# Second layer's depthwise convolution: 52 of 196 taps on GpSimd, VectorE's partial sums in PSUM, three query groups between the chunks

## The reference

```python
x_ln = layernorm(x, ln_g, ln_b)
q = x_ln @ wq + bq                                  # query image, one per channel
o = conv_general_dilated(q_img, dw_w, (2, 2), [(3, 3)] * 2, feature_group_count=c)   # 7x7, depthwise, stride 2
o = gelu(o + dw_b)                                  # 16x16 points
offsets = 1x1 conv of o with pw_w                   # 2 numbers a point
grid = tanh(offsets) and the reference points
interp = bilinear samples of x at grid              # 256 points
k, v from interp; q again through mq_w; attention; mo_w; residual; layernorm; mlp_w; gelu; residual
```

## Time and profile before

| | |
|---|---|
| time, median of 3 runs | 4248.88 us (4244.26 to 4249.75) |
| the profiled execution | 4248.9 us, span 4247.2 us |
| mean granted clock of TensorE | 0.984 of full |
| busy: TensorE, VectorE, ScalarE, GpSimd | 4062.9, 2985.9, 2580.8, 1303.4 us |
| VectorE's taps (L1537), 880 | 363.7 us |
| TensorE's taps (L1203), 656 of two passes | 324.1 us in the records |
| ScalarE's diagonals (L1382), 656 | 250.6 us |

### The profile page before, as it was taken

The page is one execution under the profiler, slowest core; times in us unless marked ns, Lnnn a source line. Parts: engine busy times, 40 slices in busy tenths (PEclk is TensorE's granted clock), DMA queues, the critical chain, the costliest instruction groups (busy, mean ns, idle before and its releaser), DMA issues. The chain is left out here.

```text
span 4247.2 us, 65056 instructions
## 1 busy us (share of the span) xinstructions
PE 4062.9 (96%) x22762; PEld 3395.2 (80%) x22762; DVE 2985.9 (70%) x5141; ACT 2580.8 (61%) x5617; POOL 1303.4 (31%) x1423
## 2 busy tenths in 40 slices
PE   8999999999999999999999889999999999999999
PEld 6887878878878878788788577777777777777777
DVE  3983965956938839749569466859686868686866
ACT  3874855847828738558478136565656555555656
POOL 1431423432323324324323104132232314140504
PEclk9999999999999999999999989999999999999999
DMA  2221121221211211212211303031212121212212
GB/s 82 43 66 43 41 75 35 61 61 31 56 56 41 68 43 41 70 41 61 60 31 36 138 1 100 20 80 40 70 50 60 60 60 60 60 60 49 72 38 63
DMA packets 113159, 235.87 MB, mean 56 GB/s; under 512 B 17261, under 2 KB 33705, under 8 KB 112809
## 3 DMA queue, kind: packets, MB, share of 16 engines
q1 hardware_dynamic: 112808, 231.41, 20.4%
HBM read 80.35 MB, written 33.55 MB: 27 GB/s over the span
## 5 line engine op out<-in xcount | busy, mean ns | idle before, releaser
L599 DVE TENSOR_REDUCE a_neg_max<-a_ps 128x1 f32<-128x1024 f32 x512 | 624.7, 1221 | 337.1 <-PE a_ps L429 337.1
L558 ACT ACTIVATE a_ph<-a_ps 128x512 fp32r<-128x512 f32 x1024 | 556.9, 593 | 171.4 <-PE a_ps L443 168.5
L616 DVE TENSOR_TENSOR a_pl<-a_ps,a_ph 128x512 fp32r<-128x512 f32 x1024 | 654.2, 679 | 8.9 <-ACT a_ph L558 5.7
L565 ACT ACTIVATE a_prob<-a_ps,a_neg_max 128x1024 f32<-128x1024 f32 x512 | 572.3, 1118 | 17.5 <-DVE a_neg_max L599 11.8
L696 POOL TENSOR_TENSOR a_qk<-a_fold_s,a_fold_r 64x256 f32<-64x256 f32 x256 | 191.1, 747 | 1237.1 <-DVE a_fold_s L607 1237.1
L443 PEld LDWEIGHTS a_ps<-a_ident,a_prob 128*128 128x128 f32 x4096 | 469.8, 140 | 112.8 <-issue 47.0
L443 PE MATMUL a_ps<-a_ident,a_prob 128*128 128x128 f32 x4096 | 540.7, 274 | 17.3 <-DVE a_pl L616 16.2
L1697 POOL TENSOR_SCALAR b_prob<-b_prob,b_row_inv 128x256 f32<-128x256 f32 x512 | 246.7, 482 | 994.9 <-DVE b_row_inv L1606 959.0
L464 PE MATMUL a_ps<-a_ph,a_v 128*128 128x256 f32 x2048 | 550.7, 302 | 0.0
L464 PE MATMUL a_ps<-a_pl,a_v 128*128 128x256 f32 x2048 | 509.2, 282 | 0.0
L428 PE MATMUL a_ps<-a_kh,a_qs 128*128 128x512 f32 x1024 | 408.3, 399 | 11.9 <-POOL a_kl L687 11.9
(11 more groups left out here) (250 smaller groups left out, 9239.3 us busy)
## 6 DMA issues: line engine op xcount, KB each, us to landing
a_qs<-a_qk SPq DMA_DIRECT2D x128, 256.0 KB, 3.7
a_kl<-a_qk SPq DMA_DIRECT2D x128, 256.0 KB, 4.3
a_xtok<-in_x SPq DMA_DIRECT2D x64, 256.0 KB, 4.2
b_xs<-x SPq DMA_DIRECT2D x64, 256.0 KB, 4.6
b_qs<-b_qh SPq DMA_DIRECT2D x64, 256.0 KB, 3.0
b_qs<-b_ql SPq DMA_DIRECT2D x64, 256.0 KB, 3.8
b_z<-x SPq DMA_DIRECT2D x64, 256.0 KB, 3.2
out<-b_ot SPq DMA_DIRECT2D x64, 256.0 KB, 2.0
```

The source lines that it names most:

```text
L558: act.activation(ph[:, b % 2, 4 * g:4 * g + 4, (u % 2) * P:(u % 2 + 1) * P], ps[:, 4 + n % 2, :].rearrange("p (k q) -> p k q", k=4), ACT.C ...
L565: act.activation(prob[:, i_ % 2, :], ps[:, 2 * (i_ % 2):2 * (i_ % 2) + 2, :] .rearrange("p a b -> p (a b)"), ACT.Exp, bias=neg_max[:, i_:i ...
L599: dve.tensor_reduce(neg_max[:, i_:i_ + 1], ps[:, 2 * (i_ % 2):2 * (i_ % 2) + 2, :] .rearrange("p a b -> p (a b)"), AX, ALU.max, negate=Tru ...
L616: dve.tensor_tensor(pl[here], ps[:, 4 + n % 2, :].rearrange("p (k q) -> p k q", k=4), raw(ph[here]), ALU.subtract).then_inc(pl_ok, 1)
```

## The change

The core of the diff; in the part of `convolve` the instructions stand in the order PE_SUM, POOL_SUM, taps:

```diff
-    DVE_TAPS = [29, 29, 28, 28]
+    PAIRS = ((0, 1), (2, 3))
+    POOL_TAPS = [12, 12, 14, 14]
+    DVE_TAPS = [29, 23, 22, 22]
+    PRODUCTS = 9
     SOLO = 20
-    left = [[(c, n) for n in range(DVE_TAPS[c])] + [(c, None)] for c in range(CT)]
+    PE_SUM, POOL_SUM = -1, -2
+    first_dve = POOL_TAPS
+    first_pe = [POOL_TAPS[c] + DVE_TAPS[c] for c in range(CT)]
+    left = [[(c, n) for n in range(first_dve[c], first_pe[c])] + [(c, PE_SUM), (c, POOL_SUM)] for c in range(CT)]
     taps = [left[0].pop(0) for _ in range(SOLO)]
...
+    pool_ops = [2 * POOL_TAPS[x] for x, y in PAIRS]
+    act_taps = [(d, j, w) for d, (x, y) in enumerate(PAIRS) for j in range(1, POOL_TAPS[y]) for w in range(2)]
+    pe_taps = [(c, n) for c in range(CT) for n in range(first_pe[c], KS * KS)]
...
+        prod = E.take("b_prod", [P, PRODUCTS, NS])
...
-        QH_BANK = (4, 5, 6, 0, 1, 2, 4, 5)
-        IT_BANK = (7, 3)
-        K_BANK = (6, 3, 7, 2)
+        QUERY_BEHIND = (0, 2, 3)
+        QH_BANK = (4, 5, 0, 7, 2, 3, 4, 5)
+        IT_BANK = (1, 6)
+        OFF_BANK = 1
+        K_BANK = (6, 7, 2, 3)
...
             def queries(groups):
                 for g in groups:
+                    if g < 2:
+                        pe.wait_ge(q_sb, at(q_sb, CT + g + 1))
+                    if g == 2:
+                        pe.wait_ge(tap, at(tap, taps_upto[0]))
...
-            pe.wait_ge(q_sb, at(q_sb, 2 * CT))
-            queries(range(3))
-
+            for e, (c, n) in enumerate(pe_taps):
+                first, last = n == first_pe[c], n == KS * KS - 1
+                if first:
+                    pe.wait_ge(q_sb, at(q_sb, CT + c + 1))
+                pe.wait_ge(dg_ok, at(dg_ok, e + 1))
+                mm = pe.matmul(ps[:, c, 0:NS], diag[:, e % DIAGS, :], window(c, n), start=first, stop=last)
+                mm.then_inc(dg_used, 1)
+                if last and c in QUERY_BEHIND:
+                    queries((QUERY_BEHIND.index(c),))
+
+            pe.wait_ge(tap, at(tap, taps_upto[1]))
...
+            def product(a):
+                d, j, w = act_taps[a]
+                c = PAIRS[d][w]
+                if a >= PRODUCTS:
+                    d0, j0, w0 = act_taps[a - PRODUCTS]
+                    act.wait_ge(ptap, at(ptap, pool_count(d0, j0, w0 + 1)))
+                act.wait_ge(q_sb, at(q_sb, CT + c + 1))
+                act.activation(grid(prod[:, a % PRODUCTS, :]), window(c, j), ACT.Copy, scale=dww[:, c, j:j + 1])\
+                   .then_inc(prod_ok, 1)
+
+            rest, behind = len(act_taps) - PRODUCTS, len(pe_taps) - DIAGS
+            for a in range(PRODUCTS):
+                product(a)
             for e in range(DIAGS, len(pe_taps)):
                 act.wait_ge(dg_used, at(dg_used, e - DIAGS + 1))
                 diagonal(e)
+                for a in range(PRODUCTS + rest * (e - DIAGS) // behind, PRODUCTS + rest * (e - DIAGS + 1) // behind):
+                    product(a)
             for c in range(CT):
                 act.wait_ge(tap, at(tap, taps_upto[c]))
-                act.activation(o[:, c, :], acc[:, c, :], ACT.Gelu).then_inc(gelu_ok, 1)
+                act.activation(o[:, c, :], acc[:, c, :], ACT.Gelu, bias=vec[:, 28 + c:29 + c]).then_inc(gelu_ok, 1)
...
-                    if n is None:
+                    if n == PE_SUM:
                         dve.wait_ge(dg_used, at(dg_used, pe_upto[c]))
-                        dve.tensor_tensor(acc[:, c, :], ps[:, c, 0:NS], acc[:, c, :], ALU.add).then_inc(tap, 1)
+                        dve.tensor_tensor(o[:, c, :], ps[:, c, 0:NS], o[:, c, :], ALU.add).then_inc(tap, 1)
...
+                    if n == POOL_SUM:
+                        dve.wait_ge(ptap, at(ptap, pool_count(c // 2, POOL_TAPS[c] - 1, 2)))
+                        dve.tensor_tensor(acc[:, c, :], acc[:, c, :], o[:, c, :], ALU.add).then_inc(tap, 1)
...
+                    partial = ps[:, 6 + c // 2, c % 2 * NS:c % 2 * NS + NS]
+                    dst = grid(o[:, c, :] if n == first_pe[c] - 1 else partial)
...
-                        dve.scalar_tensor_tensor(dst, src, dww[:, c, n:n + 1], dst, ALU.mult, ALU.add)\
+                        dve.scalar_tensor_tensor(dst, window(c, n), dww[:, c, n:n + 1], grid(partial), ALU.mult,
+                                                 ALU.add).then_inc(tap, 1)
...
+            for d, (x, y) in enumerate(PAIRS):
+                for j in range(POOL_TAPS[x]):
+                    if j == 0:
+                        pool.wait_ge(q_sb, at(q_sb, CT + x + 1))
+                        pool.tensor_scalar(grid(acc[:, x, :]), window(x, j), dww[:, x, j:j + 1], 0.0, ALU.mult,
+                                           ALU.add).then_inc(ptap, 1)
...
+                    for w, c in enumerate((x, y)):
+                        a = act_taps.index((d, j, w))
+                        pool.wait_ge(ptap, at(ptap, pool_count(d, j - 1, w + 1)))
+                        pool.wait_ge(prod_ok, at(prod_ok, a + 1))
+                        pool.tensor_tensor(acc[:, c, :], acc[:, c, :], prod[:, a % PRODUCTS, :], ALU.add)\
+                            .then_inc(ptap, 1)
```

More of the change, by code:

```diff
@@ L748, in layer1 @@
     tap_before = [max([m + 1 for m in range(k) if taps[m][0] == taps[k][0]], default=0) for k in range(len(taps))]
-    taps_upto = [taps.index((c, None)) + 1 for c in range(CT)]
-    pe_taps = [(c, n) for c in range(CT) for n in range(DVE_TAPS[c], KS * KS)]
+    taps_upto = [taps.index((c, POOL_SUM)) + 1 for c in range(CT)]
+    pool_ops = [2 * POOL_TAPS[x] for x, y in PAIRS]
+    act_taps = [(d, j, w) for d, (x, y) in enumerate(PAIRS) for j in range(1, POOL_TAPS[y]) for w in range(2)]
+    pe_taps = [(c, n) for c in range(CT) for n in range(first_pe[c], KS * KS)]
     pe_upto = [sum(e[0] <= c for e in pe_taps) for c in range(CT)]
@@ L804, in layer1 @@
         assert t_at + 16384 <= SB_END
-        qpad = Region(nc, q_at, l_at).take("b_qpad", [P, CT, PADW * PADW])
+        E = Region(nc, q_at, l_at)
+        qpad = E.take("b_qpad", [P, CT, PADW * PADW])
+        prod = E.take("b_prod", [P, PRODUCTS, NS])
         E = Region(nc, t_at, SB_END)
@@ L1118, in layer1, with window, grid, pool_count @@
         EACH.update({s.num: 64 for s in o_st})
-        EACH.update({dg_ok.num: len(pe_taps), dg_used.num: len(pe_taps), tap.num: len(taps), off_ps.num: 1,
+        EACH.update({dg_ok.num: len(pe_taps), dg_used.num: len(pe_taps), tap.num: len(taps), ptap.num: sum(pool_ops), prod_ok.num: len(act_taps), off_ps.num: 1,
                      tanh_ok.num: 1, xy_ok.num: 3, hy_ok.num: TT + 2})
         steps = [0]
+        def window(c, n):
+            dy, dx = n // KS, n % KS
+            return qpad[:, c, :].rearrange("p (y x) -> p y x", x=PADW)[
+                :, dy:dy + 2 * GRID - 1:2, dx:dx + 2 * GRID - 1:2]
+        def grid(ap):
+            return ap.rearrange("p (y x) -> p y x", x=GRID)
+        def pool_count(d, j, n):
+            return sum(pool_ops[:d]) + 2 * j + n
         def counted(r):
@@ L1225, in tensor_image @@
                         pe.wait_ge(gelu_ok, at(gelu_ok, k + 1))
-                    mm = pe.matmul(ps[:, 7, c * NS:(c + 1) * NS],
+                    mm = pe.matmul(ps[:, OFF_BANK, c * NS:(c + 1) * NS],
                                    vec[:, 20 + 4 * c + k:21 + 4 * c + k].to_broadcast([P, P]), o[:, k, :],
```

35 lines of the change are left out of this document (11 added, 24 removed).

## The result

The changed kernel takes 4266.16 us (median of six runs, 4264.02 to 4269.48), the kernel before 4249.63 us over six (4244.26 to 4251.19). The ratio is 1.0041, with a 95% interval from 1.0028 to 1.0054: the change made the kernel 16.5 us slower, where 62 us less had been forecast. The profiled execution took 4269.5 us, its span is 4267.7 us.

A forecast was written before the change was run, and what follows sets the result against it. TensorE, busy 96%, was taken as the bound, then VectorE's and GpSimd's end. Offsets 10.0 us earlier, less 2.2 for the clock, give 7.8 an image; 8 x 7.8 - 0.4 = 62 off 4248.9: 4187 us, range 4165 to 4245.

The forecast's parts named there:

- rival (b): VectorE and GpSimd block each other on two-SBUF-input instructions; if every addition hit a tap, over 4400 us; 0.05 shared with slow additions.
- TensorE, 34 taps less: Convolution stage: diagonal taps fall from 82 to 48, 16.6 us less; TensorE ready for the offsets at 2966.0.
- met long before: Queries 0 to 2 on TensorE: their waits, chunk 0's finished sum included, were to cost nothing.
- VectorE's end: Convolution stage: VectorE's last three sums begin at 2971.5, with taps still 0.392 us apart plus a PSUM cost.
- The 10 ns a tap for PSUM: VectorE's taps with partial sums in PSUM: 10 ns more each, 1.0 us in all.
- (c): A VectorE tap with its sum in PSUM no longer overlaps the one before: gain 1.8 us an image, 4235; chance 0.07.
- (d): VectorE's reads and writes of one PSUM bank take turns, 268 ns more a tap: 4367 us; chance 0.08.
- GpSimd: Convolution stage: 48 additions of 0.743 us, 0.80 apart, ending at 2970.7, level with VectorE.
- ScalarE: Convolution stage: 34 diagonals fewer, 48 products more, 0.31 us each; some 30 us in a stage of 48, no bound.
- the ring: Nine slots for products: ScalarE waits for a free one and runs at GpSimd's pace, 0.98 us a diagonal.
- The clock: TensorE idles some 6 us before the offsets; 11 of 16 offset matmuls run at half clock, losing 2.2 us an image.
- called it free: Bias given inside ScalarE's gelu: no extra cost, 4 instructions as before.

The follow-up runs named there:

- e2: Changed kernel, but GpSimd waits before each addition for the one right before it, not the one before that; sum keeps two SBUF inputs: 4189.68 us.
- e8: Changed kernel, but every eighth GpSimd addition waits for the one right before it, leaving a gap there: 4179.87 us.
- e10: Changed kernel with one gap an image: the first addition of GpSimd's second train, ahead of chunk 0's sum, waits for its predecessor: 4177.69 us.
- e4: Changed kernel with VectorE's partial sums in SBUF instead of PSUM, so each tap has two SBUF inputs: 4351.89 us.
- e1: Changed kernel, but VectorE's running sum stays in PSUM up to the last step, so that sum has only one SBUF input: 4176.43 us.
- e9: Changed kernel with one gap an image: the fifteenth addition of GpSimd's second train, behind chunk 0's sum's arrival, waits for its predecessor: 4198.26 us.
- e3: e1 with query group 2 made three times over (24 matmuls more an image) to fill TensorE's idle time: 4160.26 us.
- e5: e1 with six taps moved from VectorE to TensorE (VectorE 29, 21, 20, 20): 4138.97 us.

## Why the prediction was wrong, step by step

- **The step that failed** stands under rival (b): "only the sums with GpSimd's part are of the first, one of which (chunk 0's) meets GpSimd at work, up to 0.75 us". The instruction, its place and its condition were right. The price was not: 10.95 us an image instead of 0.75 at most, and not even that stood in the sum. It was read off meetings with a single addition (1434 instead of 683 ns; 14 of the 64 subtractions have it), ahead of which GpSimd had been idle for 2 us or more, and carried over to a train of 26. No row of before shows a meeting in the middle of a train; the L624 rows above lie at a train's start. In e2, e8 and e10 the sum takes 0.41 to 0.91 us: there the forecast price holds.
- Rival (b) was called as good as dead because the taps keep clear of it. The taps do: 481 ns each over 704, though GpSimd works beside most of them. That part held, and e4 shows what it is worth.
- **TensorE, 34 taps less**: right. In e1 it is done with query 2 35.4 us after the evacuation (2956.92 - 5.33 - 2916.18), forecast 35.9. In the changed kernel query 2 itself waited 2.5 to 2.9 us for the stalled sum in every image, a wait which the prediction had called met long before.
- **VectorE's end**: the last three sums begin 2988.04 - 2937.47 = 50.6 us after the evacuation instead of the forecast 40.9. Without the stall of 10.95 it is 39.6, as e1 has it (2955.80 - 2916.18). The 10 ns a tap for PSUM were not there: the last 34 taps start 0.39 us apart (13.40 us), as in the earlier trace rows.
- **Rivals (c) and (d)**: dead. A tap with its sum in PSUM is 481 ns against 478 and overlaps the next as before. The Trainium skill, VectorE: DVE Perf Modes, section on the TRN2 errata, gives 120 cycles of fixed cost for a PSUM source against 58. The trace disagrees: as for the input alone, no such difference shows where a tap both reads and writes the bank.
- **GpSimd**: one addition 0.748 us long in the mean, 0.743 forecast, but 0.694 apart instead of 0.80. The gap taken from multiplications isn't there; the additions overlap, as those of layer 0 did in the trace of before (L705 above: 1.27 long, the next 1.23 behind), which the prediction didn't use. The end came 34.9 us after the evacuation instead of 40.1. This mis-sized term did no harm by itself, but the gapless train is a condition of the stall (e2, e9).
- **ScalarE**: products are 0.44 us apart, not 0.31, and never wait for the ring, since GpSimd is quicker than thought. Done at 2968.4, they are no bound in the changed kernel. ScalarE's timeline:

```profile
2937.50 3.59 ACT L1427 ACTIVATE b_prod<-b_qpad,b_dww 128x256 f32<-128x256 f32 x8 [2.72 <-DVE b_qpad L1589]
```

- **The clock**: mechanism right. The forecast loss was 2.2 us; e1 has 2.35 with its 5.4 us of idle time, the changed kernel 3.04 in the third image, where the granted clock is at half for all but the last of the offsets. 0.2 of the 3.04 is not the clock: at full clock the offsets take 3.83 us with the new gelus (e3, e5) against 3.61 before. The forecast's 0.226 us for a matmul of 512 columns at full clock was taken from the offset matmuls, which have 256; that it fits (L901 in the changed kernel: 0.227 apart) is luck.

Term by term for one image: forecast a gain of 7.8 us, measured a loss of 2.7, a difference of 10.5. The stall gives 10.95, the offset matmuls 0.84 more, the earlier end of VectorE's own work takes 1.3 back: 10.5. Without the stall (e1) the forecast of 4187 would have been 11 us too high, 1.3 us an image.

## What to carry to other kernels

Ask of every VectorE instruction with two SBUF inputs whether a long, gapless train of GpSimd two-input instructions runs beside it: its price can then be the rest of the train, not one instruction, and it pushes back all that VectorE has queued. One operand in PSUM removes it at no cost (89.7 us here). Where that can't be had, a wait of GpSimd on its own predecessor before every addition bounds it to the addition in hand (76.5 us here); a single such wait ahead of the meeting gave 88.5 us in one run, but why it did is open, so that it may fail elsewhere. Then look at who stands idle: TensorE's 5 us before the offsets cost twice, in time and in clock, and six taps moved to it gave 37 us more.

## What the runs showed of the hardware

- A VectorE instruction of 0.41 us can be shut out for 11.36 us by 16 GpSimd additions, and a tap of 0.47 for 15.94 us. Two SBUF inputs and additions without gaps are both needed (e1, e2) and not enough: e8 and e10 and layer 0 of the kernel before have both at the meeting, and there VectorE gets in at the end of the addition in hand.
- A gap while VectorE waits lets it in: 3.07 us, until GpSimd's next wait on its predecessor (e9).
- When VectorE's two-input instructions follow one another from before the train's start, the engines alternate (e4: 0.86 and 0.88 us apart), and GpSimd's additions grow from 0.75 to some 0.91 us.
- GpSimd's 128x256 additions start 0.694 us apart and last 0.72 to 0.81; with a wait on the predecessor before each they are 0.81 apart (e2).
- VectorE reads and writes a PSUM bank in one instruction at no price: 481 ns, 0.39 us apart.
- A gelu with a bias of its own for each channel takes 500 ns in the mean of 32, against 406 of 32 before the change. The prediction had called it free.
